# Head-size-8 attention stages: the exponential goes first on ScalarE, and the norm's rounding and split follow one step later

## What is computed

```python
h1 = _ln(x, n1_g, n1_b)
x = _attn(h1, h1, q1, k1, v1, o1_w, o1_b, heads) + x
h2 = _ln(x, n2_g, n2_b)
x = _attn(h2, context, q2, k2, v2, o2_w, o2_b, heads) + x

# _attn, dh = 8
sim = jnp.einsum('bhid,bhjd->bhij', q, k) * scale
a = jax.nn.softmax(sim, axis=-1)
out = jnp.einsum('bhij,bhjd->bhid', a, v)
out = out.transpose(0, 2, 1, 3).reshape(b, n, heads * dh)
return out @ wo + bo
```

## Time and profile before

| | us |
|---|---|
| median of 3 runs | 4061.24 (4060.48 to 4071.21) |
| the profiled execution | 4059.68 |
| its span | 4057.9 |
| busy: PE, PEld | 3848.0 (95%), 3327.7 (82%) |
| busy: DVE, ACT, POOL | 2323.5 (57%), 2166.9 (53%), 1215.0 (30%) |
| stage a0, from the first norm work to the last output | about 20 to 525 |
| stage c0 | about 525 to 1175 |

### The profile page before, as it was taken

The page is one execution under the profiler, slowest core; times in us unless marked ns, Lnnn a source line. Parts: engine busy times, 40 slices in busy tenths (PEclk is TensorE's granted clock), DMA queues, the critical chain, the costliest instruction groups (busy, mean ns, idle before and its releaser), DMA issues. The chain is left out here.

```text
span 4057.9 us, 101732 instructions
## 1 busy us (share of the span) xinstructions
PE 3848.0 (95%) x38592; PEld 3327.7 (82%) x38592; DVE 2323.5 (57%) x4208; ACT 2166.9 (53%) x5452; POOL 1215.0 (30%) x1313
## 2 busy tenths in 40 slices
PE   5999979999979979999999999979999999999899
PEld 3777757777769969888898888868888888888798
DVE  3677534434335546666666666645555555556555
ACT  3677545555434455555555555545555555555444
POOL 3122031111024423333333333322222222222443
PEclk7899855555569989999999999989999999999999
DMA  3333222122110010000000000000000000000000
GB/s 101 91 94 96 62 71 59 47 62 56 50 36 0 0 42 1 0 0 0 0 0 0 0 0 0 1 24 3 2 2 2 2 2 2 2 2 1 16 19 21
DMA packets 97875, 98.56 MB, mean 24 GB/s; under 512 B 27664, under 2 KB 73104, under 8 KB 97680
## 3 DMA queue, kind: packets, MB, share of 16 engines
q1 hardware_dynamic: 94480, 94.50, 8.6%
q10 hardware_dynamic: 3200, 1.31, 0.1%
HBM read 20.76 MB, written 5.24 MB: 6 GB/s over the span
## 5 line engine op out<-in xcount | busy, mean ns | idle before, releaser
L1070 POOL TENSOR_TENSOR a_probs<-a_probs,a_rsums 128x1024 f32<-128x1024 f32 x160 | 303.6, 1898 | 750.4 <-DVE a_rsums L1168 750.4
L1090 ACT ACTIVATE a_probs<-a_scores_banks,a_negmax 128x128 f32<-128x128 f32 x1280 | 366.6, 376 | 297.6 <-DVE a_negmax L1156 297.6
L1070 POOL TENSOR_TENSOR c_probs<-c_probs,c_rsums 128x616 f32<-128x616 f32 x160 | 201.4, 1259 | 768.3 <-DVE c_rsums L1168 768.2
L1090 ACT ACTIVATE c_probs<-c_scores_banks,c_negmax 128x77 f32<-128x77 f32 x1280 | 312.0, 334 | 203.9 <-DVE c_negmax L1156 203.9
L1149 DVE COPY c_outT<-c_out_bank 128x512 f32<-128x512 f32 x160 | 110.7, 692 | 370.7 <-PE c_out_bank L1310 310.5
L1433 ACT ACTIVATE f_gate<-f_up_bank,bias 128x256 f32<-128x256 f32 x320 | 151.0, 472 | 288.2 <-PE f_up_bank L323 288.2
L1457 DVE SCALAR_TENSOR_TENSOR f_hidden<-f_up_bank,bias,f_gate 128x256 f32<-128x256 f32 x320 | 149.6, 481 | 254.8 <-ACT f_gate L1433 136.9
L1149 DVE COPY a_outT<-a_out_bank 128x512 f32<-128x512 f32 x160 | 110.6, 691 | 298.1 <-PE a_out_bank L1310 246.1
L681 ACT ACTIVATE c_probs<-c_scoresT_banks 77x1024 f32<-77x1024 f32 x160 | 163.0, 1019 | 172.2 <-PE c_scoresT_banks L800 171.9
L1156 DVE TENSOR_REDUCE a_negmax<-a_scores_banks 128x4 f32<-128x512 f32 x320 | 206.2, 686 | 73.9 <-PE a_scores_banks L1211 73.9
L738 DVE TENSOR_REDUCE a_negmax<-a_scores_banks 128x8 f32<-128x1024 f32 x160 | 195.6, 1222 | 81.7 <-PE a_scores_banks L783 80.0
(11 more groups left out here) (340 smaller groups left out, 11853.5 us busy)
## 6 DMA issues: line engine op xcount, KB each, us to landing
a_q_stack<-a_q_compact SPq DMA_DIRECT2D x96, 160.0 KB, 3.4
a_k_stack<-a_k_compact SPq DMA_DIRECT2D x96, 160.0 KB, 3.6
c_q_stack<-c_q_compact SPq DMA_DIRECT2D x96, 160.0 KB, 3.2
c_k_stack<-c_k_compact SPq DMA_DIRECT2D x96, 96.2 KB, 2.8
x_tokens<-in_x SPq DMA_DIRECT2D x16, 320.0 KB, 5.0
a_out<-a_heads SPq DMA_DIRECT2D x64, 80.0 KB, 2.5
c_out<-c_heads SPq DMA_DIRECT2D x64, 80.0 KB, 2.0
out_x<-x_tokens SPq DMA_DIRECT2D x32, 160.0 KB, 1.9
```

The costliest lines, as they stand in the source:

```text
L1070: nc.gpsimd.tensor_tensor(probs[i][:], probs[i][:], rsums[(k - 1) % 2][:].unsqueeze(2).broadcast_to([P, UNIT, NK]), ALU.mult).then_inc(s_p ...
L1090: done = nc.scalar.activation(probs[i][:, h, :], scores[:, h // GROUP, h % GROUP * NK:(h % GROUP + 1) * NK], ACT.Exp, bias=negmax[k % 2][: ...
```

## The change

In `attention_small`, ACT's exponential stands ahead of the value copy and of the norm's work within a step. `scalar_affine` is cut in two: the scale and bias stay at s = 5 and 7, and the rounding is the new `scalar_high` at s = 6 and 8, ahead of the shift. The wait for the projections that still read the old high part goes with it. DVE's low part moves from s = 6 to 7 and its stack from s = 7 to 9. The shift's rounding and DMA stay on ACT where they were, behind what now stands ahead of them. PE, POOL and SP have the same instructions in the same order. The diff:

```diff
--- before.py
+++ after.py
@@ -431,20 +431,23 @@
             last = nc.tensor.transpose(self.bank[:, a * P:(a + 1) * P], self.h[:, a, part * P:(part + 1) * P], self.m.ident[:])
         last.then_inc(self.s_hT, 1)
 
-    def scalar_affine(self, e, n, par, part, parts_used):
+    def scalar_affine(self, e, n, part):
         nc = self.m.nc
         if part == 0:
             if isinstance(n, int) and n == 0:
                 self.weights.wait_params(e)
             if due(n):
                 e.wait_ge(self.s_split, n)
-            used, count = parts_used
-            if due(count):
-                e.wait_ge(used, count)
         e.wait_ge(self.s_hT, 2 * n + part + 1)
         nc.scalar.activation(self.y[:, part, :], self.bank[:], ACT.Identity,
                              bias=self.params.norm_cols[:, 2 * part + 1:2 * part + 2],
                              scale=self.params.norm_cols[:, 2 * part:2 * part + 1]).then_inc(self.s_y, 1)
+
+    def scalar_high(self, e, n, par, part, parts_used):
+        nc = self.m.nc
+        used, count = parts_used
+        if part == 0 and due(count):
+            e.wait_ge(used, count)
         e.wait_ge(self.s_y, 2 * n + part + 1)
         nc.scalar.copy((self.yhigh if part else self.high[par])[:], self.y[:, part, :]).then_inc(self.s_high, 1)
 
@@ -654,19 +657,6 @@
                             act.wait_ge(s_stack[i], 16 * STACK_DMAS * n)
                     act.wait_ge(s_proj, 4 * n + t + 1)
                     nc.scalar.copy(compact[:, half, 0, :], (even_bank, odd_bank)[half][0:HALF, 0:width]).then_inc(s_proj_high, 1)
-                if s in (5, 7) and live(ahead, QUADS):
-                    norm.scalar_affine(act, ahead, local % 2, (s - 5) // 2,
-                                       (s_proj, 4 * (ahead - 1)) if cross else (s_vproj, 2 * (ahead - 1)))
-                values = values_at(q, k - 1)
-                if values:
-                    c, n, par = values
-                    act.wait_ge(s_vproj, 2 * n + c + 1)
-                    if isinstance(n, int) and n <= 1:
-                        act.wait_ge(s_ones, 6)
-                    if c == 0 and due(n - 1):
-                        act.wait_ge(s_pv, QUNITS * (n - 1))
-                    nc.scalar.copy(v[par][0:NK, 2 * c:2 * c + 2, :, 0:32:SPREAD],
-                                   (even_bank, odd_bank)[c][0:NK, 0:2 * D].rearrange("p (a h d) -> p a h d", a=2, h=HEADS)).then_inc(s_v, 1)
                 if cross and s == 0 and live(ahead - 1, QUADS):
                     act.wait_ge(s_ctxT, ahead)
                     if due(ahead - 1):
@@ -679,6 +669,21 @@
                     if due(n - 1):
                         act.wait_ge(s_pv, n - 1)
                     nc.scalar.activation(probs[i][0:NK, :, :], scoresT[0:NK, :, :], ACT.Exp).then_inc(s_exp, 1)
+                values = values_at(q, k - 1)
+                if values:
+                    c, n, par = values
+                    act.wait_ge(s_vproj, 2 * n + c + 1)
+                    if isinstance(n, int) and n <= 1:
+                        act.wait_ge(s_ones, 6)
+                    if c == 0 and due(n - 1):
+                        act.wait_ge(s_pv, QUNITS * (n - 1))
+                    nc.scalar.copy(v[par][0:NK, 2 * c:2 * c + 2, :, 0:32:SPREAD],
+                                   (even_bank, odd_bank)[c][0:NK, 0:2 * D].rearrange("p (a h d) -> p a h d", a=2, h=HEADS)).then_inc(s_v, 1)
+                if s in (5, 7) and live(ahead, QUADS):
+                    norm.scalar_affine(act, ahead, (s - 5) // 2)
+                if s in (6, 8) and live(ahead, QUADS):
+                    norm.scalar_high(act, ahead, local % 2, (s - 6) // 2,
+                                     (s_proj, 4 * (ahead - 1)) if cross else (s_vproj, 2 * (ahead - 1)))
                 made = maxima_at(q, k)
                 if made:
                     g, par, order, n = made
@@ -755,9 +760,9 @@
                 if s == 9 and live(quad_of(q, k) - 1, QUADS):
                     dve.wait_ge(s_sums_in, 16 * quad_of(q, k))
                     nc.vector.reciprocal(sums[:], sums[:]).then_inc(s_rsums, 1)
-                if s == 6 and live(ahead, QUADS):
+                if s == 7 and live(ahead, QUADS):
                     norm.vector_low(dve, ahead, local % 2)
-                if s == 7 and live(ahead, QUADS):
+                if s == 9 and live(ahead, QUADS):
                     norm.vector_stack(dve, ahead, local % 2)
 
             def prepare(k):
```

## The result

The changed kernel takes 4034.42 us (median of 5 runs, 4027.36 to 4035.91) where the kernel before takes 4061.24 (5 runs on the same chip, 4058.47 to 4075.84). The ratio is 0.9918 with a 95% interval of 0.99 to 0.9936: 0.8% faster. The profiled execution took 4034.42 us and its span is 4032.6, 25.3 us less than the 4057.9 of before.

A forecast was written before the change was run, and what follows sets the result against it. It took c0 as bound by PE at the low clock and a0 by one step's chain across engines. Terms -4, +1.6, -8 and +2 sum to -8.4 from 4059.7 us; forecast 4052 us, range 4015 to 4076.

The forecast's parts named there:

- Same: Whole kernel: time between 4049 and 4073 us, within the 0.3% that can't be told from no change; chance 0.43.
- rival B: c0 keeps the high clock over whole quads, 18 us less each; one to three give 4000 to 4035 us; chance 0.20.
- (1): a0 at the high clock: exponential first in steps 5 and 7 saves 0.3 us a quad, -4 us in about 13 quads.
- The sign named for a failure of (1): a0 quads still at 25.0 us instead of 24.7 would show the predicted a0 gain wrong.
- DVE's stack: a0, between reciprocal and step 0's maximum: ends at 408.75, before the maximum's present start; a 3 us loss if no slack.
- (3): c0 at the low clock: context transposes start 0.1 us later, behind the value copy; +1.6 us over 16 quads (0 to 2.5).
- (4): c0's two spells at the high clock: each lasts another 9 us or so, into step 9, saving 4 us; -8 us together.
- (5): a0's first quads: 1.1 us of held PE time comes back, but the clock's rise may come later; +2 us, 0 to 20 possible.
- Rival C: a0 misses the clock's rise at 134 us; one more low-clock quad gives 4069 to 4072 us, two 4090; chance 0.17.
- A: The forecast itself for the whole kernel: 4040 to 4060 us, 4052 likeliest; chance 0.42.
- The rule weighed in the prediction: PE's clock: low when idle, 2.4 GHz when busy, so removing idle time keeps it high once granted; c0's trace disagreed.

## Why the prediction was right or wrong

The prediction said 4052 us, from 4015 to 4076, and the time came inside it, 18 us below the point. "Same" had the larger chance, and the kernel is faster by 0.8%. What happened in the profiled execution is rival B with its smallest count, one whole quad of c0 at the high clock, which its own sum puts at 4052 - 18 = 4034. That this is the measured time is luck: the sum has a0 at -4 + 2 = -2 and c0 at 1.6 - 8 - 18 = -24.4, and by the exponentials they are -12.7 and -10.9. The steps:

- **(1), a0's quads: size right, cause wrong.** -0.3 us a quad was said, -0.36 came in the quad shown, and 4.0 us in eleven quads. Counted from step 6's scores, L818 was to start 0.40 and 0.52 us earlier in steps 6 and 8; it was 0.48 and 0.55. The sign named for a failure of (1), a quad of still 25.0 us, was set wrong: 25.0 was the count of 8 quads in 200 us of before, and by the exponentials a quad took 25.4. And I gave the gain to the exponential. The runs with either half show that the exponential alone makes the quad 25.9 us and the rounding, with DVE's two behind it, 25.0. What PE waits for in steps 6 and 8 is the last of ACT's work of steps 5 and 7, the heads copy. The early exponential by itself only exchanges a wait ahead of the transposed scores for one ahead of L823. My sum had this chain in it, with the rounding out of it, and so came out right; I read the cause from the row with the idle time and not from the sum.
- **DVE's stack: right.** It stands between reciprocal and maximum as predicted, and moving it to step 8 changes nothing.
- **(3), c0 at the low clock: right.** 39.5 us a quad instead of 39.4; with the value copy ahead of the exponential it is 39.4 again, and with it behind the heads copy 40.0.
- **(4), c0's spells: the term of the sum that was mis-sized.** "Another 9 us, then into step 9" was said, two spells, -8. One spell came, 27 us longer than before, where there had been two short ones: 26.1 - 2 x 6.8, less the 1.6 of the longer quads, is the 10.9 measured. The step that failed is the one that let the wait of step 9 end the spell. In the changed kernel PE waits for the value copy there at the high clock, for 0.90 us, and the clock stays, as it does behind the 0.58 us at 854.28:

```profile
858.09 0.31 PEld L939 LDWEIGHTS c_even_bank<-ident,c_ctx_in 77*96 77x96 f32 x4 [0.90 <-ACT c_v L680]
```

- **(5), a0's first quads: the sign was wrong.** +2 was said, with 0 to 20 possible; -9.0 came. I let the earlier matmuls only miss the rise, and did not ask whether the spell at 104 us would outlast what ended it. The first gap of the low clock behind that spell is 0, 10.2, 10.3, 10.3 and 13.7 us long in the five traces with the new order in a0 (stack in step 8 included), 3.4 without the early exponential, and none with the heads copy early; with the rounding in steps 5 and 7 it is 20.5 to 23.9 in four traces. With the transfer on SyncE it is 20.5 too. Rival C, a loss against before in these quads, is in no trace.
- **The chances.** I gave the spells that were still to be had a chance of 0.20 (B) and half of A. What spoke for B was in the rows: the idle time ahead of the fall, 0.30 us, was the one that the change removes. What I held against it, that c0's matmuls are narrower, did not keep the spell from lasting 37.5 us (PE is busy for 35.83 of them).

The rule weighed in the prediction, Trainium skill, "TensorE: Matmul & The Clock Gate", section Part 1, with the high clock for a busy PE, fares no better here: PE was busy for 589.70 of 590 us at 0.50 in c0 of the run that moves the rounding alone. The direction that rival B took from it came, a longer spell once the idle time at step 6 was gone. But it doesn't say where a spell ends either: the long spell has the smaller busy share of the two, 35.83 of 37.50 us where the short one has 9.99 of 10.20.

Where in a quad a c0 spell starts is the same in all 17 spells of the traces, whatever the order: in step 2, 0.1 to 0.4 us behind the loads for the denominators of step 1 (in the changed kernel the clock rises at 840.3):

```profile
838.47 1.53 PEld L882 LDWEIGHTS c_max_bank<-c_sums,select 80*80 80x80 f32 x7 [0.17 <-issue]
840.30 0.18 PEld L788 LDWEIGHTS c_scores_banks<-c_k_stack,c_q_stack 31*128 31x128 f32 x2 [0.30 <-issue]
```

Open stays why it comes in one quad and not in another, what ends it, and whether the new order makes one more likely. Fourteen profiled executions had 0, 1 or 2, in various quads.

## What to carry to other kernels

Where two engines exchange work in steps, count an engine's work in each step up to the last result that is waited for. Moving one instruction ahead of another, with both still ahead of that result, only exchanges the waits; moving one to a step with slack takes them away, and that was the gain of a0's quads here (25.4 to 25.0 us). Moving the awaited result itself ahead, the heads copy, gave another 0.2 to 0.4 us a quad. Where a stage runs at the low clock with PE full, look for the short spells at the high clock: the order of the instructions set their length here, and a long one is worth more than all that the order brings by itself (26 us a spell against 0.36 us a quad). The last wait ahead of a fall is a place to try, not a proven cause, since waits as long stood inside the same spells. And the spells come and go between executions, so one profile does not price a change.

## What the runs showed of the hardware

The changed kernel, profiled twice, had its c0 spell in two different quads (from 840.3 and from 799.9 us). Over kernels with the changed order in c0 or close to it, c0's time goes with the number of long spells: 546.6, 572.7 to 572.9 and 596.6 us between the first exponential and the last for two, one and none; the last is the kernel without the early exponential, whose quads take 39.4 us where the others' take 39.5. The length of a spell is the same to 0.1 us under one order: 37.5 or 37.6 us six times with the changed one, 10.2 or 10.3 six times with the rounding in steps 5 and 7. All start in step 2 of a quad.

One execution of 3903.62 us at a mean clock of 0.939 suggests that c0 can do far better. From the traces, a quad at the high clock saves 39.4 - 23.6 = 15.8 us, so 131 us would be some eight of them. That it was c0 is an estimate, since it was not profiled: a mean of 0.939 over 3901.8 us is some 476 us at the low clock, and the profiled execution of the same kernel, with 0.899, had some 815, of which 631 lie in c0 (515.1 to 1163.6 us, less the spell of 17.1) and 184 elsewhere. So some 155 or more of the 339 us that are missing must have been in c0.
